# Rows for the experts: transposed on TensorE, or as 16-bit planes by the DMA engines

## What is computed

```python
x = L0_attn_data
x = x + einsum('bsk,nk->bsn', layernorm(x), weight * block_mask)
xn = layernorm(x)
logits = xn @ W_gate + b_gate
_, top_idx = top_k(logits, 2)
y_all = relu(einsum('bsd,edh->bseh', xn, W_e) + b_e)
x = x + take_along_axis(y_all, top_idx[..., None], axis=2).mean(axis=2)
```

## Time and profile before

| | |
|---|---|
| median of 3 runs | 751.87 us |
| the profiled execution, its own time | 752.44 us |
| its span, first to last instruction | 750.7 us |
| TensorE busy (matmuls) | 712.1 us, 95% |
| VectorE, ScalarE, GpSimd busy | 325.9, 239.9, 289.6 us (43%, 32%, 39%) |
| mean granted TensorE clock | 0.982 |
| DMA | 118.22 MB, 157 GB/s |

### The profile page before, as it was taken

The page is one execution under the profiler, slowest core; times in us unless marked ns, Lnnn a source line. Parts: engine busy times, 40 slices in busy tenths (PEclk is TensorE's granted clock), DMA queues, the critical chain, the costliest instruction groups (busy, mean ns, idle before and its releaser), DMA issues.

```text
span 750.7 us, 11322 instructions
## 1 busy us (share of the span) xinstructions
PE 712.1 (95%) x3655; PEld 582.1 (78%) x3655; DVE 325.9 (43%) x645; ACT 239.9 (32%) x324; POOL 289.6 (39%) x310
## 2 busy tenths in 40 slices
PE   3999999999999739999999999999999999999994
PEld 2568888888888628888888888888888888888883
DVE  4756887887877665035063360252162360000000
ACT  2232323324223113433243332433323333233330
POOL 5622222232232115354453544535445363443420
PEclk9999999999999959999999999999999999999998
DMA  8723554545444277468577685486386673432313
GB/s 319 285 91 134 204 172 152 189 169 176 172 159 147 105 253 241 96 139 247 133 192 227 139 232 136 101 264 144 87 241 185 170 197 85 88 45 41 57 29 56
DMA packets 35653, 118.22 MB, mean 157 GB/s; under 512 B 5904, under 2 KB 5904, under 8 KB 35600
## 3 DMA queue, kind: packets, MB, share of 16 engines
q1 hardware_dynamic: 23184, 80.23, 29.9%
q0 software_dynamic: 11232, 37.23, 24.6%
q10 hardware_dynamic: 1184, 0.04, 0.1%
HBM read 83.40 MB, written 37.75 MB: 161 GB/s over the span
## 4 chain that ended last, share of the span: by engine, by line
PE 95%; DMA 2%; DVE 1%; issue 1%; POOLq 0%; ACT 0%; POOL 0%; SPq 0%; DVEq 0%; ACTq 0%
PE psO L266 81%; PE psT L416 5%; PE psG L383 2%; PE psT L301 2%; PE psO L332 1%; PE psT L293 1%; DMA xb<-L_attn_data 1%; PE psS L332 1%; PE psT L368 1%; DMA x<-x_rows,tok_of 1%; PE psG L280 0%; PE psT L319 0%; POOLq L40 0%; DVE st L562 0%; DVE xT L786 0%
## 5 line engine op out<-in xcount | busy, mean ns | idle before, releaser
L266 PE MATMUL psO<-slots,xT 128*128 x1872 | 437.4, 393 | 2.5 <-DVE xT L786 2.5
L266 PEld LDWEIGHTS psO<-slots,xT 128*128 128x128 f32 x1872 | 350.1, 189 | 74.5 <-issue 2.9
L266 PE MATMUL psO<-wT,xT 128*128 128x512 f32 x768 | 184.1, 395 | 0.0
L266 PEld LDWEIGHTS psO<-wT,xT 128*128 128x128 f32 x768 | 141.5, 188 | 29.8 <-issue 0.9
L916 POOL DMA_INDIRECT rows_out<-xb,tok_of x39 | 65.6, 1682 | 236.5 <-ACT xb L532 236.5
L665 DVE CAST slots<-raw 128x1024 fp32r<-128x1024 f32 x56 | 54.1, 966 | 214.9 <-PE psO L266 144.0
L532 ACT ACTIVATE xb<-psO 128x512 f32<-128x512 f32 x78 | 46.7, 599 | 258.4 <-PE psO L266 258.4
L909 POOL TENSOR_TENSOR xT<-x2T,xT 128x1024 fp32r<-128x1024 f32 x38 | 98.0, 2580 | 21.4 <-ACT x2T L500 21.4
L667 DVE TENSOR_TENSOR slots<-raw,slots 128x1024 fp32r<-128x1024 f32 x56 | 75.1, 1341 | 1.9
L507 ACT ACTIVATE psO<-bias_slot 128x512 f32 x78 | 46.9, 602 | 39.3 <-ACT xb L532 22.1
L447 ACT ACTIVATE xT<-psT 128x1024 fp32r<-128x1024 f32 x16 | 16.4, 1027 | 133.9 <-PE psT L301 133.9
(11 more groups left out here) (133 smaller groups left out, 446.3 us busy)
## 6 DMA issues: line engine op xcount, KB each, us to landing
raw<-L_ffn_W_e SPq DMA_DIRECT2D x56, 512.0 KB, 5.4
xb<-L_attn_data SPq DMA_DIRECT2D x16, 512.0 KB, 3.3
xr<-L_attn_data SPq DMA_DIRECT2D x16, 512.0 KB, 4.1
rows_out<-xr SPq DMA_DIRECT2D x16, 512.0 KB, 2.9
x_rows<-x SPq DMA_DIRECT2D x16, 512.0 KB, 2.9
mask_stage<-L_attn_mask SPq DMA_DIRECT2D x8, 512.0 KB, 11.9
w_stage<-L_attn_weight SPq DMA_DIRECT2D x8, 512.0 KB, 12.6
raw<-L_ffn_W_e SPq DMA_DIRECT2D x16, 256.0 KB, 3.4
```

The costliest lines, as they stand in the source:

```text
L266: last = eng.matmul(psum, xT[:, p, a, kt, :], moving(b, kt), start=(i == 0 and kt == 0 and not seeded), stop=(i == len(PASSES) - 1 and kt ...
```

## The change

The rows are stored as 16-bit planes: a row of `x2_rows` is now 2,048 numbers of 16 bits, the low halves of its 1,024 floats and then the high halves. ScalarE makes them from the normalized tile, which goes to `x2T` first. A gathered block is then a 128 x 2,048 matrix of 16-bit numbers. ScalarE's queue issues one DMA for each block that transposes it within SBUF into `turned` (16 squares of 128 x 128), and an activation joins the halves again into the float32 `x2T`. HI is copied from there, and LO is made on GpSimd for all blocks. TensorE's transposes of gathered rows, and the second copy out of PSUM, are gone.

```diff
-        x2_rows = nc.dram_tensor("x2_rows", (N_TOK, D), F32, kind="Internal").ap()
+        x2_rows = nc.dram_tensor("x2_rows", (N_TOK, 2 * D), U16, kind="Internal").ap()
...
+        turned = [sb("turned_even", [P, 2 * KT, P], U16), at("turned_odd", [P, 2 * KT, P], U16, foldedT_offset)]
+        x2n = x2T[:].rearrange("p k t -> p (k t)")
+        def planes_of(t):
+            return x2[:, t % 2, :].bitcast(U16)
...
@@ sync
-                    eng.wait_ge(c_ln2, i)
-                    eng.dma_start(x2_rows[(i - 1) * P:i * P, :], x2[:, p, :]).then_inc(l_x2[p], 16)
+                    eng.wait_ge(c_planes, i)
+                    eng.dma_start(x2_rows[(i - 1) * P:i * P, :], planes_of(i - 1)).then_inc(l_x2[p], 16)
@@ tensor
-            def transpose_rows(b):
-                eng.wait_ge(l_gather[b % 3], 16 * (b // 3 + 1))
...
-                for kt in range(KT):
-                    last = eng.transpose(psT[:, b % 2, kt, :], rows_of(b, slice(kt * P, (kt + 1) * P)), ident[:])
-                last.then_inc(c_turn, 1)
...
-                if 1 <= b and b + 1 < N_BLOCKS:
-                    transpose_rows(b + 1)
@@ scalar, for each tile
-                    eng.activation(x2[:, t % 2, :], xr[:, t % 2, :], ACT.Identity,
+                    eng.wait_ge(c_planes, t)
+                    eng.activation(x2n, xr[:, t % 2, :], ACT.Identity,
                                    bias=rs[:, 1, 2:3], scale=rs[:, 1, 1:2]).then_inc(c_ln2, 1)
+                    eng.wait_ge(c_ln2, t + 1)
+                    eng.activation(planes_of(t).rearrange("p (h d) -> p h d", h=2),
+                                   x2n.bitcast(U16).rearrange("p (d h) -> p h d", h=2), ACT.Copy).then_inc(c_planes, 1)
@@ scalar, for each block
+            def turn_rows(b):
+                eng.wait_ge(l_gather[b % 3], 16 * (b // 3 + 1))
+                if b >= 2:
+                    eng.wait_ge(c_joined, b - 1)
+                eng.dma_start_transpose(turned[b % 2][:], rows_of(b)).then_inc(l_turn[b % 2], 16)
+
+            def join_rows(b):
+                eng.wait_ge(l_turn[b % 2], 16 * (b // 2 + 1))
+                if b > 0:
+                    eng.wait_ge(c_rlo, b)
+                else:
+                    eng.wait_ge(c_planes, NB)
+                eng.activation(x2T[:].bitcast(U16).rearrange("p k (t h) -> p h (k t)", h=2),
+                               turned[b % 2][:].rearrange("p (h k) t -> p h (k t)", h=2), ACT.Copy).then_inc(c_joined, 1)
+
             def rows_hi(b):
-                eng.wait_ge(c_turn, b + 1)
+                eng.wait_ge(c_joined, b + 1)
                 if b >= 2:
                     eng.wait_ge(c_half, NH * b)
-                hi = eng.activation(xT[:, b % 2, HI, :, :], psT[:, b % 2, :, :], ACT.Copy)
...
-                eng.wait_ge(c_rlo, b)
-                eng.activation(x2T[:], psT[:, b % 2, :, :], ACT.Copy).then_inc(c_rhi, 1)
+                eng.activation(xT[:, b % 2, HI, :, :], x2T[:], ACT.Copy).then_inc(c_rhi, 1)
...
+            for b in range(2):
+                turn_rows(b)
+            join_rows(0)
             rows_hi(0)
+            turn_rows(2)
+            join_rows(1)
             for b in range(N_BLOCKS):
                 if b + 1 < N_BLOCKS:
                     rows_hi(b + 1)
+                if b + 3 < N_BLOCKS:
+                    turn_rows(b + 3)
                 if b >= 2:
                     eng.wait_ge(l_add[b % 2], 16 * (b // 2))
                 for n in range(NH):
...
                         seed_half(b + 1, slot, n)
+                    if n == 0 and b + 2 < N_BLOCKS:
+                        join_rows(b + 2)
@@ vector
-            eng.tensor_tensor(xT[:, 0, LO, :, :], psT[:, 0, :, :], xT[:, 0, HI, :, :].bitcast(F32), ALU.subtract).then_inc(c_rlo, 1)
@@ gpsimd
             def gather_rows(b):
                 if b >= 3:
-                    eng.wait_ge(c_turn, b - 2)
+                    eng.wait_ge(l_turn[(b - 3) % 2], 16 * ((b - 3) // 2 + 1))
...
+            eng.wait_ge(c_ln2, NB)
+            eng.memset(x2_third[:], 0.0).then_inc(c_clear, 1)
...
+            def rows_lo(b):
+                eng.wait_ge(c_rhi, b + 1)
+                eng.tensor_tensor(xT[:, b % 2, LO, :, :], x2T[:], xT[:, b % 2, HI, :, :].bitcast(F32), ALU.subtract).then_inc(c_rlo, 1)
+
             for b in range(3):
                 gather_rows(b)
+            rows_lo(0)
             for b in range(N_BLOCKS):
                 if b + 1 < N_BLOCKS:
-                    eng.wait_ge(c_rhi, 2 * (b + 2))
...
+                    rows_lo(b + 1)
                 if b + 3 < N_BLOCKS:
                     gather_rows(b + 3)
```

More of the change, by code:

```diff
@@ L9 @@
 I32 = mybir.dt.int32
+U16 = mybir.dt.uint16
 ALU = mybir.AluOpType
@@ L53, in sb @@
                 size *= s
-            size *= 2 if dt == F16 else 4
+            size *= 2 if dt in (F16, U16) else 4
             t = at(name, shape, dt, cursor[0])
@@ L98, in build @@
         ones = sb("ones", [P, P], F32)
+        foldedT_offset = cursor[0]
         foldedT = sb("foldedT", [N_EXP, NH, HALF], F32)
@@ L137, in build, with rows_of @@
         x2_third = at("x2_third", [P, D], F32, xr_offset + D * 4)
-        assert cursor[0] <= xr_offset + D * 4 and end <= nc.sbuf_usable_end
-        def rows_of(b, cols=slice(0, D)):
-            return x2_third[:, cols] if b % 3 == 2 else x2[:, b % 3, cols]
+        assert cursor[0] <= xr_offset + D * 4
+        cursor[0] = end
+        turned = [sb("turned_even", [P, 2 * KT, P], U16), at("turned_odd", [P, 2 * KT, P], U16, foldedT_offset)]
+        assert cursor[0] <= nc.sbuf_usable_end
+        x2n = x2T[:].rearrange("p k t -> p (k t)")
+        def planes_of(t):
+            return x2[:, t % 2, :].bitcast(U16)
+        def rows_of(b):
+            return (x2_third[:] if b % 3 == 2 else x2[:, b % 3, :]).bitcast(U16)
         def ps(name, shape, dt=F32):
@@ L184, in build @@
         c_hi0, c_lo0, c_split = sem("c_hi0"), sem("c_lo0"), sem("c_split")
-        c_turn, c_rhi, c_rlo, c_half = sem("c_turn"), sem("c_rhi"), sem("c_rlo"), sem("c_half")
+        l_turn = even_odd("l_turn")
+        c_planes, c_joined, c_clear = sem("c_planes"), sem("c_joined"), sem("c_clear")
+        c_rhi, c_rlo, c_half = sem("c_rhi"), sem("c_rlo"), sem("c_half")
         c_out, c_seed = sem("c_out"), sem("c_seed")
@@ L407, in _ @@
             eng.sem_inc(c_half, NH)
-            def transpose_rows(b):
-                eng.wait_ge(l_gather[b % 3], 16 * (b // 3 + 1))
[L411 to L414, removed]
-                for kt in range(KT):
-                    last = eng.transpose(psT[:, b % 2, kt, :], rows_of(b, slice(kt * P, (kt + 1) * P)), ident[:])
-                last.then_inc(c_turn, 1)
             eng.wait_ge(c_lo0, NB)
-            transpose_rows(0)
             eng.wait_ge(c_tab_d, 15)
             for b in range(N_BLOCKS):
-                if 1 <= b and b + 1 < N_BLOCKS:
-                    transpose_rows(b + 1)
                 s = eng.value_load(slot_of[0:1, b:b + 1], min_val=0, max_val=1)
@@ L433, in _ @@
                     products(psO[:, n, :], b % 2, moving, True).then_inc(c_half, 1)
-                    if b == 0 and n == 0:
-                        transpose_rows(1)
         @block.scalar
@@ L781, in _ @@
             eng.wait_ge(c_mm, NH * NB)
-            for kt in range(2):
-                split_chunk(1, kt)
-            eng.wait_ge(c_rhi, 2)
-            eng.tensor_tensor(xT[:, 0, LO, :, :], psT[:, 0, :, :], xT[:, 0, HI, :, :].bitcast(F32), ALU.subtract).then_inc(c_rlo, 1)
-            for kt in range(2, KT):
+            for kt in range(KT):
                 if kt == KT - 1:
@@ L900, in _ @@
                 eng.wait_ge(l_x2[p], 16 * (NB // 2))
+            eng.wait_ge(c_ln2, NB)
+            eng.memset(x2_third[:], 0.0).then_inc(c_clear, 1)
             eng.wait_ge(s_spare, 16)
+            eng.wait_ge(c_clear, 1)
             eng.wait_ge(c_tab_d, 11)
+            def rows_lo(b):
+                eng.wait_ge(c_rhi, b + 1)
+                eng.tensor_tensor(xT[:, b % 2, LO, :, :], x2T[:], xT[:, b % 2, HI, :, :].bitcast(F32), ALU.subtract).then_inc(c_rlo, 1)
             for b in range(3):
                 gather_rows(b)
+            rows_lo(0)
             for b in range(N_BLOCKS):
                 if b + 1 < N_BLOCKS:
-                    eng.wait_ge(c_rhi, 2 * (b + 2))
-                    p = (b + 1) % 2
-                    eng.tensor_tensor(xT[:, p, LO, :, :], x2T[:], xT[:, p, HI, :, :].bitcast(F32), ALU.subtract).then_inc(c_rlo, 1)
+                    rows_lo(b + 1)
                 if b + 3 < N_BLOCKS:
```

## The result

The changed kernel takes 962.3 us (median of 4 runs, 958.1 to 966.9) beside 752.0 us for the kernel before: a ratio of 1.280, 95% interval 1.273 to 1.286. The profiled execution has a span of 965.2 us; 964.1 were forecast.

A forecast was written before the change was run, and what follows sets the result against it. PE bounds the kernel before; the changed one was to hang on a loop through the gather's landing: 304.3 + 30 x 18.1 + 5 x 15.1 = 922.8, then PE's tail, span 964.1, forecast 965 us; range 873 less 13 to 1082 rounded up.

The forecast's parts named there:

- The new wait: Block loop: ScalarE's transposing DMA waits for a gather that can't be early behind LO, so PE runs out of seeded PSUM.
- The turn: Block loop, second ReLU to second ReLU: 15.2 us plus the transposing issue; 18.1 us for 30 blocks, 15.1 for five.
- The term c: Time the transposing DMA's issue holds ScalarE's queue in each turn: 2.9 us taken, bounds 0.47 and 5.2.
- The scatter and LO: GpSimd's part of each turn: 2.67 us from ReLU to LO's start, then 2.73 from LO's start to the gather's.
- The join: ScalarE's activation joining the 16-bit halves in each block: 1.83 us and 0.1 of wait; bounds 1.2 and 3.7.
- The start: Ahead of the loop: PE starts block 0 at 285.7, not 278.36; block 0's second ReLU ends at 304.3.
- The projection: One more ScalarE activation per tile, 1.83 us; gate copy moves to about 203.4, hidden with 0.7 us to spare.
- TensorE's clock: PE idles some 7 us each turn, so the lower clock may return; a block then takes 13.4 us, still hidden.
- The two rules of the Trainium skill: Price of the transposing issue: as fast as regular DMAs would give 873 us; the cycle table 3.4 us, 984 in all.
- Cheap issue: Rival: the transposing DMA's issue costs 0.47 us, saving 92 us against the forecast: about 873 us; chance 0.25.
- Dear issue: Rival: the issue costs 5.2 us or more, or transfers crowd gathers: 1052 us, 1082 with later landings; chance 0.29.
- The faster case: Rival: the gather's wait is hidden behind PE, 33 us go and block 0's start gives back 7: 726 us; chance 0.03.

The follow-up runs named there:

- the version with the early gather: Changed kernel, with GpSimd issuing the gather of block b+3 ahead of the LO part of block b+1: 932.8 us, ratio 1.241 to the kernel before.
- the plain DMA: Changed kernel with a plain DMA of the same bytes in place of the transposing one, rows not transposed: 890.1 us, ratio 1.184 to the kernel before.
- the late issue: Changed kernel, with ScalarE issuing each block's transposing DMA one iteration later (block b+2 in iteration b): 807.7 us (783.0 to 819.1).
- the late issue with plain DMAs: Changed kernel with the DMA issued one iteration later and plain instead of transposing, same bytes: 727.5 us, ratio 0.967 to the kernel before.
- held weights: Changed kernel, transposing DMA issued one iteration later, SyncE loading expert 1's weights only after the first two transposing DMAs land: 819.1 us (793.1 to 827.7).

## Why the prediction was right

The forecast was 965 us and the runs gave 962.3; the reason was right, the sizes of the terms less so than the sum looks.

- **The new wait.** Right, and shown: with the transposing DMA moved behind the gather's landing, the wait goes and the time falls by 155 us.
- **The turn.** 30 x 18.1 + 5 x 15.1 was 17.7 on the mean, measured 17.3. The term c was 1.85 us, not 2.9, the landing 4.5, not 5.2. The other way went the join, 2.48 us and not 1.83, and the two readings of the table, 0.9 us longer, which I had at their old price. The too-high and the too-low terms cancel in part: from the second ReLU of block 0 to that of block 35 it was 602.7 us, 16 less than the forecast's 618.5.
- **The scatter and LO.** I had LO start 0.20 us after the scatter's instruction, 2.67 us after the ReLU. The bracket of that row names L500, a copy that the change removes, as what LO waited for. In the changed kernel LO starts 0.48 us before the scatter's instruction ends, 2.0 us after the ReLU on the median. It takes 2.89 us on the mean there, not 2.58, but 2.40 on the median in the version with the early gather, where it doesn't stand behind the scatter. So the scatter's term was 0.6 too high and LO's 0.3 too low, both from one overlap.
- **The join.** It writes 16-bit elements at a stride of two. The other activation of 2,048 such elements, L477, reads at that stride and writes without gaps, and took 1.91 us, near the 1.83. So the 0.65 too few go with the strided write. (L503 first, then L477, ns min/median/max.)

```profile
L503 ACT ACTIVATE x2T<-turned_even x20: 2481/2482/2510, 289.8 to 929.0; 128x2048 uint16<-128x2048 uint16 x20
```

```profile
L477 ACT ACTIVATE x<-x2T x16: 1910/1911/1912, 62.9 to 262.3; 128x2048 uint16<-128x2048 uint16 x16
```

- **The start.** This term was mis-sized most: the second ReLU of block 0 ended at 318.8, forecast 304.3. I gave the first two transposing DMAs 2.9 us each and a landing of 5.2. The timeline has:

```profile
275.17 5.91 ACTq L495 DMA_TRANSPOSE turned_even<-x  x1
281.13 8.43 ACTq L495 DMA_TRANSPOSE turned_odd<-x  x1
289.81 2.48 ACT L503 ACTIVATE x2T<-turned_even 128x2048 uint16<-128x2048 uint16 x1 [16.73 <-DMA turned_even<-x]
```

The first landed 14.6 us after its issue. The third held ScalarE for another 8.14 us, to 300.53, where I had it hidden behind LO 0. SyncE issues six weight loads between us 265 and 292, with landings of up to 16.3 us, and with the loads held back the first issues were shorter (above). I had written that the transfer's own time isn't on the path; for block 0 it is. The 14.5 us too few of the start and the 16 us too many of the turns cancel, by chance: the second ReLU of block 35 ended at 921.5, forecast 922.8.

- **The projection.** Right: the split took 1.91 us, the gate copy moved to 202.81 and its reader at 203.82 didn't wait.
- **TensorE's clock.** It came as described: the granted clock was 0.86 on the mean of us 320 to 650, between its two levels, and a matmul took 435 ns on the mean where it took 393. It cost nothing in the turns, since the first ReLU always stood behind the DMA. PE's share was 78% and not 70%, since the same matmuls lasted longer.
- **The two rules of the Trainium skill.** What the Trainium skill says in Advanced Engine Details and Errata, X-Bar Transpose (TRN2), that transposing DMAs are as fast as regular ones, does not hold here: 1.85 us of issue against 0.48, 4.3 us to landing against 2.9, 3.0 us of all engines against 1.4. The Trainium skill's cycle table in DMA: Bandwidth & Descriptors, section on why a DMA increments its semaphore by 16, gave an estimate of 3.4 us of issue, and the measured 1.85 is about half of it; the tile size I put in was a guess.
- **The rivals.** Cheap issue (873 us) is what the plain DMA does, 890 us. Dear issue, "or the transfers crowd the gathers", didn't come at 17 us a turn; with the late issue the transfers do crowd each other, once the loop runs faster beside the weight loads. The faster case, 726 us with the wait hidden, is the 727.5 us of the late issue with plain DMAs, and real transposing DMAs miss it by some 80.

## What to carry to other kernels

Ask of a DMA that waits in a compute engine's queue what stands behind it, and follow the thing it waits for through every other queue to see whether it can be early; three buffers for the gather were worth nothing here, since its issue stood behind LO. Before moving work from TensorE to the DMA engines, add up their time for one block at the pace you hope for: 7.6 us plus 3.0 us left next to nothing of 10.9 us, though the engines' mean share of 0.65 looked like room. And where a forecast hits, check its terms: here two errors of some 15 us hid each other.

## What was not expected of the hardware

- Transposing DMAs beside weight loads slow each other far beyond what the bytes say: landings of 22 to 28 us for all of them at 90 GB/s in one stretch of 28 us, where the plain form of the same program had 4.5 us for its loads and 275 GB/s in that stretch.
- ScalarE's small reads from a table behind its own DMA issue take up to 0.98 us on the median where they took 0.28.
- A gather issued right behind a scatter on GpSimd's queue (0.31 us after its instruction) lands 1.8 us later than one issued 2.6 us after it.
- The issue of a transposing DMA lasts longer where the DMA engines are busy, up to 8.4 us in the changed kernel and 13.6 with held weights, against 1.3 to 1.9 for most. So ScalarE seems to be held by other queues' traffic. Why is open; no run took it apart.
